# A scan layer with two feed-forward blocks on one core: four edits to a hand-written order of steps

## The reference, cut to what matters

```python
h   = x + mamba2(rmsnorm(x) * ln1_w)            # w_in, conv of 4 taps, silu, scan over 4 chunks of 128, w_out
h2  = rmsnorm(h) * ln2_w
x1  = layernorm(x + h + silu(h2 @ gate.T) * (h2 @ up.T) @ down.T)
out = layernorm(x1 + ternary_ffn(x1))
# inside mamba2, for each chunk c of a batch (4 heads of 128, state of 128):
dt  = softplus(dt_raw + dt_bias);  a = dt * (-exp(A_log));  cs = cumsum(a)
att = (C @ B.T) * exp(cs_q - cs_k) (lower triangle) ;  Yd = att @ (X * dt)
state_c = g * state_(c-1) + B.T @ (X * dt * decay_to_end);  Yo = C @ state_(c-1) * exp(cs)
y   = ((Yd + Yo) + D * X) * silu(z);   out = y @ w_out.T
```

## Time and profile before

| what | value |
|---|---|
| median of 3 runs | 470.66 us (469.86 to 471.52) |
| the profiled execution, its own time | 470.33 us |
| its span, first to last instruction | 468.6 us |
| mean granted TensorE clock | 0.997 |
| busy: PE / DVE / ACT / POOL | 98% / 73% / 55% / 47% |
| instructions | 6392 |

### The profile page before, as it was taken

The page is one execution under the profiler, slowest core; times in us unless marked ns, Lnnn a source line. Parts: engine busy times, 40 slices in busy tenths (PEclk is TensorE's granted clock), DMA queues, the critical chain, the costliest instruction groups (busy, mean ns, idle before and its releaser), DMA issues.

```text
span 468.6 us, 6392 instructions
## 1 busy us (share of the span) xinstructions
PE 457.9 (98%) x2078; PEld 368.2 (79%) x2078; DVE 340.9 (73%) x592; ACT 259.9 (55%) x509; POOL 222.0 (47%) x275
## 2 busy tenths in 40 slices
PE   7999999999999999999999999999999999999995
PEld 6877677876777878888788888888887777788885
DVE  3674787745788897686898999974867666587275
ACT  5798867878557767555442353322708666658000
POOL 5493555406641497777878200035028455742022
PEclk9999999999999999999999999999999999999998
DMA  6720222021322425443313347620200010000022
GB/s 206 290 90 0 92 90 69 8 90 38 91 90 90 136 67 192 149 156 113 135 51 130 136 136 225 193 76 1 90 1 0 0 47 23 1 1 1 0 91 90
DMA packets 14576, 40.81 MB, mean 87 GB/s; under 512 B 2384, under 2 KB 2640, under 8 KB 14544
## 3 DMA queue, kind: packets, MB, share of 16 engines
q1 hardware_dynamic: 14544, 40.41, 25.9%
HBM read 38.30 MB, written 2.10 MB: 86 GB/s over the span
## 4 chain that ended last, share of the span: by engine, by line
PE 82%; ACT 6%; DVE 5%; issue 2%; SPq 2%; DMA 2%; POOL 1%; POOLq 0%; DVEq 0%
PE psA L1771 7%; PE psA L1773 7%; PE psA L1786 6%; PE psA L1788 5%; PE psA L1777 4%; PE psA L1779 4%; PE psB L2024 3%; PE psB L2023 3%; PE psB L2020 3%; PE psB L1786 2%; PE psB L1788 2%; PE psB L2111 2%; PE psB L2112 2%; PE psA L2024 2%; PE psA L2020 2%
## 5 line engine op out<-in xcount | busy, mean ns | idle before, releaser
L821 POOL TENSOR_SCALAR var<-mv 128x1 f32<-128x1 f32 x16 | 4.2, 266 | 107.6 <-DVE mv L1326 103.8
L886 POOL TENSOR_TENSOR beta<-wsum,beta 128x512 fp32r<-128x512 f32 x28 | 36.2, 1314 | 21.3 <-ACT beta L1094 21.3
L1215 ACT ACTIVATE c<-c 128x512 f32<-128x512 f32 x14 | 8.8, 632 | 46.7 <-DVE c L1553 46.7
L1452 DVE SCALAR_TENSOR_TENSOR xbc<-psA,convw_sb,xbc 128x511 f32<-128x511 f32 (+2 forms) x36 | 26.9, 747 | 6.8 <-ACT xbc L1153 6.0
L1754 PE MATMUL psA<-xT_h,win_h 128*128 128x512 f32 x72 | 28.5, 402 | 0.0
L1225 ACT ACTIVATE act_hl<-act 128x512 fp32r<-128x512 f32 x28 | 17.0, 627 | 18.4 <-PE psB L2024 12.2
L1756 PE MATMUL psA<-xT_l,win_h 128*128 128x512 f32 x68 | 26.6, 391 | 0.0
L1012 POOL TENSOR_TENSOR int_l<-int,int_h 128x512 fp32r<-128x512 f32 x11 | 14.3, 1296 | 18.0 <-ACT int_h L1296 18.0
L1771 PE MATMUL psA<-xT_h,beta 128*128 128x512 f32 x56 | 22.0, 393 | 0.6 <-DVE act L1569 0.3
L1603 DVE TENSOR_TENSOR act_hl<-act,act_hl 128x512 fp32r<-128x512 f32 x28 | 19.0, 686 | 4.0 <-ACT act_hl L1225 4.0
L1773 PE MATMUL psA<-xT_l,beta 128*128 128x512 f32 x56 | 21.8, 389 | 0.0
(11 more groups left out here) (360 smaller groups left out, 1600.7 us busy)
## 6 DMA issues: line engine op xcount, KB each, us to landing
raw<-in_f_gu_t SPq DMA_DIRECT2D x22, 512.0 KB, 3.5
raw<-in_w_gu_t SPq DMA_DIRECT2D x14, 512.0 KB, 3.9
raw<-in_f_dn_t SPq DMA_DIRECT2D x10, 512.0 KB, 3.4
raw<-in_w_gu_t SPq DMA_DIRECT2D x14, 256.0 KB, 2.9
raw<-in_w_dn_t SPq DMA_DIRECT2D x7, 512.0 KB, 3.4
raw<-in_w_in_t SPq DMA_DIRECT2D x5, 512.0 KB, 5.5
x<-in_hidden SPq DMA_DIRECT2D x8, 256.0 KB, 5.4
out<-x SPq DMA_DIRECT2D x7, 256.0 KB, 2.0
```

The lines of the kernel that those rows point to most:

```text
L886: nc.gpsimd.tensor_tensor(beta[:, f % 2, 1, cols], wsum[:, f % 2, cols], beta[:, f % 2, 0, cols].bitcast(F32), ALU.subtract).then_inc(gb_l ...
L1452: add = nc.vector.scalar_tensor_tensor(out=xbc[b][:, j, back:L], in0=bank_a(job)[:, 0:L - back], scalar=convw_sb[:, j, TAPS - 1 - back:TAP ...
```

## The change

Four edits of the order, one of the count of warm-up transposes, and one semaphore more. The transposes of tile 3 come behind `halfhigh(0)`, with 20 warm-up transposes in place of 24. `scale1(4)` goes ahead of `norm1(6)` and `norm1(7)`, and `scale1(5)` ahead of the load of input weights 4. `silu(0,5)` goes ahead of `inproj(0,7)`, and of the silu on its result. Batch 1's `dtturn` goes from behind `inproj(0,9)` to behind `decay(0,1)` and `until(0,2)`; `dtlog` behind `conv(1,0)`; `dtend` from behind `chunk(0,1)` to behind `conv(1,1)`. `p7` waits for the first of the two instructions of `tlast` alone, and the wait for the second goes to `p4`.

```diff
--- before.py
+++ after.py
@@ -79,20 +79,26 @@
     steps += [("norm1", t) for t in range(NC)]
 
 
-    steps += [("turn1", 0), ("turn1", 1), load("in", 0), ("turn1", 2), ("turn1", 3), ("halfhigh", 0), ("halfhigh", 1),
+    steps += [("turn1", 0), ("turn1", 1), load("in", 0), ("turn1", 2), ("halfhigh", 0), ("turn1", 3), ("halfhigh", 1),
               ("halflow", 0), ("halflow", 1), ("low1",)]
     steps += [load("in", 1), ("prepare",), load("in", 2)]
     parts = scan_parts(0)
     for j in range(NX + NZ):
         before, after, last = parts.pop(0) if j >= NX + NZ - 2 else ([], [], [])
+        if j == NX + 1:
+
+            before = before + [("silu", 0, j - 2)]
         steps += before + [("inproj", 0, j)]
         if j == 1:
             steps.append(("dt", 0))
+
+        if j in (1, 2):
+            steps.append(("scale1", NC + j - 1))
         if j in (0, 1):
             steps += [("norm1", NC + 2 * j), ("norm1", NC + 2 * j + 1)]
         if j in (0, 2):
             steps.append(load("in", 3 + j // 2))
-        if 1 <= j <= NC:
+        if 2 < j <= NC:
             steps.append(("scale1", NC + j - 1))
         if NC <= j < NX + 1:
             steps.append(("turn1", j))
@@ -104,14 +110,12 @@
         if j == NX:
 
             steps += [("dtturn", 0), ("dtlog", 0), ("dtend", 0), ("until", 0, 0)]
-        if 2 <= j < NX + 2:
+        if 2 <= j < NX + 1:
             steps.append(("silu", 0, j - 2))
         if j in (NX + 1, NX + 2):
             steps.append(load("out", j - NX - 1))
         if j == NX + NZ - 2:
             steps.append(("dt", 1))
-        if j == NX + NZ - 1:
-            steps += [("dtturn", 1), ("dtlog", 1)]
         steps += after + [("conv", 0, j)] + last
 
     sums = [("sumgu", f) for f in range(FF)] + [("sumdn", p) for p in range(FF // 2 + 1)]
@@ -122,10 +126,16 @@
             early, middle, _ = later.pop(0)
             before, after = before + early, after + middle
         convolve = j < NX and j % 2 == 1
-        steps += before + ([("conv", 1, j - 1)] if convolve else []) + [("inproj", 1, j)] + after
-        if j == 0:
+        if j == 1:
+
+            before = before + [("dtturn", 1)]
+        steps += before + ([("conv", 1, j - 1)] if convolve else [])
+        if j == 1:
+            steps.append(("dtlog", 1))
+        steps += [("inproj", 1, j)] + after
+        steps += ([("conv", 1, j)] if convolve else []) + last
+        if j == 1:
             steps.append(("dtend", 1))
-        steps += ([("conv", 1, j)] if convolve else []) + last
         if j in (2, 4, 6):
             steps += [("silu", 1, j - 2), ("silu", 1, j - 1)]
         if j in (0, 1, 2, 3, 5, 7):
@@ -321,7 +331,7 @@
 A22_SLOTS = 3
 ACT_SLOTS = 4
 
-WARM_UP = 24
+WARM_UP = 20
 KEEP_WARM = {1: 4, 2: 2}
 IN_ON_DVE = 2
 INPROJ = [n for n, w in enumerate(LOADS) if w[0] == "in"]
@@ -565,6 +575,7 @@
         t3_ready = sem("t3_ready")
         t3_high = sem("t3_high")
         t3_low = sem("t3_low")
+        t3_mlp_low = sem("t3_mlp_low")
         t4_ready = sem("t4_ready")
         t4_high = sem("t4_high")
         t4_low = sem("t4_low")
@@ -1369,7 +1380,7 @@
                     c = at[0]
                     v.wait_ge(t_rest, c + 1)
                     nc.vector.tensor_tensor(xT_l[:, 0:2, chunk(NC + c)], t_f[:, 3],
-                                            xT_h[:, 0:2, chunk(NC + c)].bitcast(F32), ALU.subtract)
+                                            xT_h[:, 0:2, chunk(NC + c)].bitcast(F32), ALU.subtract).then_inc(t3_mlp_low, 1)
                     nc.vector.tensor_tensor(tT_l[:, 2, :, chunk(c)], t_f[:, 2],
                                             tT_h[:, 2, :, chunk(c)].bitcast(F32), ALU.subtract).then_inc(t_low, 1)
                 elif kind == "load" and LOADS[at[0]][0] == "ga":
@@ -1993,7 +2004,7 @@
                 elif kind == "p7":
 
                     f = at[0]
-                    pe.wait_ge(t_low, 2 * NC)
+                    pe.wait_ge(t3_mlp_low, NC)
                     pe.wait_ge(gb_low, 2 * f + 2)
                     product(open_a(("p74", f)), sum_weights(f, 0), moving_x(1, 0), True, None)
                 elif kind == "p3":
@@ -2003,6 +2014,7 @@
                 elif kind == "p4":
 
                     f = at[0]
+                    pe.wait_ge(t_low, 2 * NC)
                     pe.wait_ge(a22_low, f + 1)
                     pe.wait_ge(c22_ready, f + 1)
                     product(bank_a(("p74", f)), a22[:, f % A22_SLOTS], moving_t(2), False, None)
```

## The result

| | before | after |
|---|---|---|
| median of 12 runs | 469.87 us (469.18 to 471.52) | 471.62 us (471.03 to 472.20) |
| the profiled execution, its own time | 470.33 us | 471.27 us |
| its span | 468.6 us | 469.5 us |

What follows compares the result with a forecast made beforehand. PE, busy 98% of the span, bounds the kernel, so only its waits count. 470.33 + 2.4 (dt edits) - 0.4 (p7) = 472.3 us, 472.7 on the median's scale; stated 472.4, range 469.9 to 473.8.

Steps and rivals of the forecast that it cites:

- my own case: Whole kernel: dt edits 2.4 us slower, p7 0.4 us gained; 471.6 to 473.6 us, chance 0.52.
- Slower begins at 472.1: A measurement of this kernel can tell about 0.3%, 1.4 us, from no change, so slower begins at 472.1 us.
- The start, `scale1`, `silu`: Warm-up, tile scaling and silu(0,5) edits: nothing in the end; silu's up to 0.48 us is taken back by POOL.
- The cap: At y of chunk 0, which needs POOL's L979: PE can gain 0.44 us there and no more.
- The gain: dt of batch 1 moved, wait for the first state's copy gone: PE 0.85 us ahead at inproj(1,1).
- The cost on DVE: Thirteen small instructions (2.67 us) and 1.6 us of waits for POOL added to 7.10 us of work before the state update.
- PE's waits: PE 0.9 us behind at chunk 2, 1.5 at outproj(0,1), 2.2 at chunk 3; 0.2 added for what follows.
- The table: ACT reloads a 1.28 us table before the exponential of chunk 2, which with its late queue comes 2.7 us late.
- no lock: Rival: POOL does not hold the small DVE instructions in their new places; 471.1 us, chance 0.2.
- `p7`: At p7(0), the wait for L1373 goes: 0.4 us gained, bounds 0.26 and 0.5 us.
- The signs: Timeline: two held instructions of 0.9 us, update ending past 68 us, waits at chunks 2 and 3, table load, L1903 at 14.2.

Runs made afterwards that it cites:

- start_only: Kernel before with 20 warm-up transposes and the first half products ahead of the transposes of tile 3; ratio 1.0 (0.999 to 1.001).
- order_only: Kernel before with only the moves of scale1(4), scale1(5) and silu(0,5); ratio 1.0002 (0.9994 to 1.0011).
- dt_only: Kernel before with only the three dt steps of batch 1 moved; ratio 1.0049 (1.0036 to 1.0061).
- behind_state: Changed kernel with dtturn(1) back in its old place, dtlog(1) and dtend(1) behind state(0,0), ahead of chunk 1; 467.97 us, 0.9961 against before.
- table_only: Kernel before plus one ScalarE logarithm of a constant behind conv(1,1), DVE untouched; ratio 1.0027 (1.0017 to 1.0037).
- p7_only: Kernel before with only p7 waiting for the first instruction of tlast(3) and p4 for the second; ratio 0.9987 (0.9978 to 0.9996).
- dtend_late: Changed kernel with the six instructions of dtend(1) behind the update of the state; ratio 1.0016 (1.0007 to 1.0025) against before.
- dtlog_ahead: Changed kernel with dtlog(1) directly behind dtturn(1), where POOL has four instructions in a row; ratio 1.009 (1.0076 to 1.0104) against before.

## Why the prediction was right, point by point

Forecast: 472.4 us, slower; measured 471.62, inside the range, at the low edge of the 471.6 to 473.6 of my own case. The difference predicted was 2.0 us and the measured one is 1.8. The median of before with more runs is 469.87, 0.5 us below the execution from which I counted, and by it the sum of 2.4 - 0.4 gives 471.9. "Slower begins at 472.1" fell with the same base: with twelve runs each, 1.8 us is clear of no change (1.0029 to 1.0048).

**The start, `scale1`, `silu`: 0.** Right (`start_only`, `order_only`). In the profile after, PE's first product with low weights started at 13.72, 0.5 us sooner, against the prediction's 14.2; that is no effect of the edit, since `start_only` had 14.15 with the same edit and the product follows DVE's `low1` in every trace. My reason for `silu`, that POOL takes back what PE gains there, is seen in the rows: y of chunk 0 started 0.49 us behind the end of POOL L979 before and starts 0.15 us behind the end of L990 (50.60) after, with a wait of 0.33 us for it. The cap is 0.34 us, not 0.44. In `dt_only`, which has no edit of `silu`, y is as close behind POOL (50.70 against 50.55); there the four transposes that left the stretch did it. Either edit reaches the cap, and together they gain no more.

**The gain: 0.85 us ahead at `inproj(1,1)`.** Measured from POOL's end to `inproj(1,1)`: 56.08 - 51.59 = 4.49 us before, 54.35 - 50.60 = 3.75 after, 0.74 ahead. The 0.1 us missing is that of the cap; from y to `inproj(1,1)` it is 0.40, as I had it. `behind_state`, which keeps the gain and has the transposes ahead of the chunk, where they cost nothing, has 1.20 us in S.

**The cost on DVE: 11.37 us from `wend` to the update.** Measured 66.42 - 55.45 = 10.97. Two waits for POOL, 0.75 and 0.73 us (0.92 and 0.90 less the 0.17 of their neighbours), 1.48 against my 1.6. The second was not on `dtlog`'s first instruction but on its second: the first started at 60.16, between two of POOL's (59.19 + 1.04 and 60.19), and got through. The thirteen cost 2.4 us of their own (10.97 - 7.10 - 1.48), not 2.67, as the last of each group overlaps what follows. I had the update end at 68.75 and it ends at 67.54, but in this execution all is 0.99 us sooner from the end of L979 on. Counted from that end it is 16.94 us after and 14.87 before (66.46), so 2.1 us later, against my 2.3: the stretch is 0.4 us shorter, and DVE enters it 0.2 us later than I had it.

I overlooked that the hold was paid in the old place too. Of `dtlog(1)` two were held there, besides the third of `dtturn(1)`:

```profile
51.91 0.72 DVE L1423 TENSOR_SCALAR dtw<-dtw 128x16 f32<-128x16 f32 x1 [0.28 <-ACT dtw L1142]
52.66 0.96 DVE L1426 SCALAR_TENSOR_TENSOR dtw<-dtw 128x16 f32<-128x16 f32 x1
```

They end at 52.63 and 53.62, 0.04 and 0.03 us behind POOL's two of `until`. The three lose 2.2 us there, ahead of the copy of the first state, and the two in the new place 1.5. What the move changed is not that small instructions are held but which bank stands behind them.

**PE's waits.** I had 1.8 us lost at L1929 of chunk 2 (68.8 less 66.7 and 0.3); it is 1.35. At `outproj(0,1)` I had 0.6 more; from L1765 at 68.87 to it (72.49) are 3.62 us, from 69.12 to 72.22 before 3.10: 0.5. At chunk 3 I had 0.7; it is 0.74. For what follows I added 0.2; up to `outproj(0,2)` it is 0.3 (83.63 to 87.06, 3.43 us, against 82.64 to 85.74, 3.10). In sum 0.85 + 2.4 = 3.25 us from `inproj(1,1)` on was predicted, 3.05 measured (87.06 - 54.35 = 32.71 against 85.74 - 56.08 = 29.66). Net of the gain the dt edits cost 2.3 us (`dt_only`) where I had 2.4. Step by step, counted from the end of L979 in each trace, PE is 0.74 us ahead at `inproj(1,1)`, then 0.7 behind past chunk 2's wait, 1.3 at `outproj(0,1)`, 2.0 at chunk 3 and 2.3 at `outproj(0,2)`; I had 0.85 ahead and 0.9, 1.5, 2.2 and 2.4 behind. No step is off by more than 0.25 us, so the mechanism held along the way and not only in the total.

**The table: 2.7 us late.** The exponential starts at 70.39, 1.53 us later than before on the clock of the trace and 2.5 us later from the end of L979 (19.79 against 17.27): close to what I had. The table's own share, 1.28 us, is as predicted, and `table_only` puts 1.3 us (S: 0.93) on the clock for it alone. In "no lock" I had 1.2 us left for it.

**`p7`: 0.4 us.** `p7_only` measured 0.6 (interval 0.2 to 1.0), and after shows the product that is L1771 of before at 170.45 without a wait: from the product ahead to the one behind are 0.45 us (170.23 to 170.68), against 0.99 (168.77 to 169.76): 0.54. The bounds, 0.26 and 0.5, were a little low. Not foreseen: in the profile of `p7_only` two later waits took it back.

**The signs.** The table, the waits at chunk 2 and chunk 3 and the two that had to go are there. Three were not as I wrote them: the update ends at 67.54 and not past 68, for the early start of this execution; the second held instruction is `dtlog(1)`'s second; the first L1903 starts at 13.72.

## What to carry to other kernels

Before moving small work off a wait, ask which bank the work behind it frees, and count the slack there: here 0.64 us of wait was bought with work that lay ahead of a bank with 1.1 us of slack. Ten small instructions cost nothing in a wait of the engine (`behind_state`), and beside a busy GpSimd one takes up to 1.06 us where it takes 0.17 alone. A move of an activation function moves the table as well, and the price falls on the next instruction that wanted the old one; count tables along ACT's queue, not only their number.

## What the runs showed of the hardware that was not expected

- A small instruction of DVE can slip in between two of POOL's that stand 0.05 us or less apart: L1434 at 60.16 took 0.17 us, with until_h's end at 60.23 and until_l's start at 60.19. The same is seen in `dt_only` (60.11) and `dtend_late` (60.77), each time 0.03 to 0.04 us ahead of until_l's start. In `dtlog_ahead` none of the four did; they came 0.10 to 0.40 us behind the start of an instruction of POOL.
- The held instruction ends 0.02 to 0.04 us behind POOL's, whether that takes 1.04 or 1.29 us: its price is about what is left of POOL's instruction when it comes, less its own 0.17.
- After PE had been idle for 3.12 us its granted clock fell to 0.50 and was back at 74.2 us (`dtlog_ahead`); behind the waits of 1.1 us or less in after it reads 1.00. By its mean clock of 1.0 the fifth execution had no such fall, so a long wait can cost more than its own length but does not always.
- The early part of the program differs by more than 1 us between executions of kernels that are the same up to there (the first chunk at 42.30 us in `dt_only`, at 43.34 in `table_only` and before), by the arrival of one transfer, while S, between two points of one trace, agrees to 0.04 us. A shift of one start between two traces is no evidence of an edit; a stretch within each trace is.
